# Host-side layouts for the inputs, and the expansion of the softmax weights shared by two engines

## The reference

```
q = layernorm(x) @ Wq.T + bq;  k = ctx @ Wk.T + bk;  v = ctx @ Wv.T + bv
per row (token): reshape q, k, v to 16 heads x 16
  logits[i, j] = q[i] . k[j] / 4        # head i against head j of the SAME row
  out[i] = sum_j softmax_j(logits)[i, j] * v[j]
out: transposed so that heads come before rows, reshaped to (128, 256), @ Wd.T + bd
x = x + out
h = layernorm(x); gates = softmax((h @ w_red) @ normalized(wg).T)   # 8 experts
o = gelu(h @ W1[e] + b1[e]) @ W2[e] + b2[e], e = argmax(gates)      # 256 -> 512 -> 256
x = x + o * max(gates)
```

## Time and profile before

| | |
|---|---|
| Median of 3 runs | 428.82 us (426.50 to 429.31) |
| The profiled execution | 430.04 us |
| Its span, first to last instruction | 428.1 us |
| TensorE busy | 381.1 us, 89% |
| VectorE busy | 310.9 us, 73% |
| POOL busy | 297.2 us, 69% |
| ScalarE busy | 234.8 us, 55% |
| Mean granted clock of TensorE | 0.979 of full speed |
| DMA | 59.31 MB, 97433 packets |

### The profile page before, as it was taken

One profiled execution on the slowest core, in us unless ns is written; L12 is line 12 of the kernel. 1 busy time (PEld: TensorE's weight loads), 2 busy tenths in 40 slices (PEclk: granted clock), 3 DMA queues, 4 the chain that ended last, 5 costly groups with the idle time before them and its releaser, 6 DMA issues.

```text
span 428.1 us, 11390 instructions
## 1 busy us (share of the span) xinstructions
PE 381.1 (89%) x3791; PEld 303.4 (71%) x3791; DVE 310.9 (73%) x667; ACT 234.8 (55%) x783; POOL 297.2 (69%) x399
## 2 busy tenths in 40 slices
PE   6996999999999989998888687978999999999980
PEld 6774676676766657565555466767999999999970
DVE  3746899899998989999999665579456555555640
ACT  4443778787686877776752564571344444444420
POOL 2767678787687877776775964656387777787751
PEclk9999999999999999999999899999899999999996
DMA  7696866978779787886566501131022222222200
GB/s 163 207 264 164 228 173 209 268 193 239 184 211 260 190 229 181 230 209 175 133 155 185 154 27 39 52 116 48 29 64 75 64 75 74 61 69 65 65 17 0
DMA packets 97433, 59.31 MB, mean 139 GB/s; under 512 B 70366, under 2 KB 88447, under 8 KB 97376
## 3 DMA queue, kind: packets, MB, share of 16 engines
...
...
## 4 chain that ended last, share of the span: by engine, by line
PE 34%; DMA 24%; DVE 14%; issue 9%; SPq 9%; POOL 7%; ACT 2%; DVEq 1%; ACTq 0%; POOLq 0%
DMA qkv_scr<-qkv 21%; PE bQ L1107 14%; PE bKV L1075 8%; PE bL L1075 7%; SPq L248 4%; POOL kx L374 3%; SPq L252 2%; SPq L283 2%; DMA b2b<-in_L_ffn_wg 2%; DVE qkv L485 2%; PE bT L1089 2%; DVE qkv L492 1%; DMA ql<-qkv_scr 1%; PE bO L1057 1%; POOL r L420 1%
## 5 line engine op out<-in xcount | busy, mean ns | idle before, releaser
L374 POOL TENSOR_TENSOR kx<-ql,mask 128x2048 f32<-128x2048 f32 x32 | 117.6, 3675 | 42.7 <-issue 32.9
L1107 PE MATMUL bQ<-w,wA 128*128 x312 | 74.3, 381 | 3.4 <-DVE r L721 2.8
L475 DVE TENSOR_TENSOR ax<-bA,mask 128x2048 f32<-128x2048 f32 x32 | 73.3, 2290 | 0.6 <-PE bA L1013 0.6
L1107 PEld LDWEIGHTS bQ<-w,wA 128*128 128x128 f32 x312 | 56.2, 190 | 10.6 <-issue 4.5
L924 PE MATMUL bKV<-wA,xcT 128*128 128x512 f32 x128 | 60.2, 593 | 0.0
L397 POOL DMA_INDIRECT out<-r,isc x39 | 41.3, 1059 | 22.3 <-issue 13.4
L420 POOL DMA_INDIRECT r<-row_scr,ig x39 | 40.5, 1038 | 6.0 <-issue 2.4
L862 ACT ACTIVATE wA<-bL,r 128x128 f32<-128x128 f32 x76 | 21.6, 367 | 41.3 <-PE bL L1075 26.7
L862 ACT ACTIVATE wA<-bKV,r 128x128 f32<-128x128 f32 x80 | 22.8, 367 | 36.1 <-issue 18.8
L355 POOL TENSOR_TENSOR rs<-ve,half 128x2 f32<-128x2 f32 x39 | 28.3, 726 | 20.3 <-ACT ve L742 20.2
L932 PE MATMUL bL<-kx,pad 128*32 128x128 f32 x1024 | 35.8, 282 | 6.8 <-POOL kx L374 6.8
...
## 6 DMA issues: line engine op xcount, KB each, us to landing
...
```

The lines of the kernel that those rows point to most:

```text
L374: eng.tensor_tensor(block(kx[:, z % 2, :]), spread_heads(ql[z % 2][:, :, 0:HD]), mask_b, ALU.mult).then_inc(S["kx"], 1)
L475: eng.tensor_tensor(block(ax[:, :]), spread_heads(bA[:, 0:C].rearrange("p (l i) -> p l i", l=NH)), mask_b, ALU.mult).then_inc(S["ax"], 1)
L1107: i_ = eng.matmul(bQ[:, 0:C], hT[b % 2][:, k, :], w2[:, bass.ds(eb * (KH * C) + k * C, C)], start=(k == 0), stop=(k == KH - 1))
```

## The change

The host now also passes `x` and context transposed, interleaved as `xc` (for each pair of tiles and partition 4 KB in a row), the weights transposed (`wkvT`, `wqT`, `wdT`, `w_redT`, `wgT`), W1 with b1 appended (`W1b`) and W2 as the kernel holds them. `xc` is loaded into `xcT`, which has place for four tiles, two tiles at a time, beside `x` in its own layout. TensorE's turns of tiles and weights and the copies behind them go, with the load of the context. The mean of Wq is now taken off by two matmuls with a matrix of -1/256 (`mean`) and one addition on VectorE. POOL finishes the variance (`ve`) in place of ScalarE, in an instruction of its own whose end it waits for. `SHARE = 3`: of the eight blocks of `ax` VectorE writes the last five, and ScalarE the first three, in three instructions after VectorE's (`scalar_expand`, waits for `ax0`). In ScalarE's step it stands behind the moments of `cat` and ahead of `scalar_ahead` and `oT`. This holds for all 32 tiles.

```diff
--- before.py
+++ after.py
-CT = 6
+XC = 4
...
+SHARE = 3
...
+        xcT = r1[:, 0:XC * 4 * P].rearrange("p (n a c) -> p n a c", n=XC, a=4)
...
-            for w, src in ((1, Wk), (2, Wv), (0, Wq)):
-                eng.dma_start(wst[w], src.rearrange("(a p) c -> p a c", p=P)).then_inc(S[f"ld_w{w}"], 16)
+            eng.dma_start(wT[:, :, 0:2 * C], wkvT).then_inc(S["ld_wkv"], 16)
+            eng.dma_start(wT[:, :, 2 * C:3 * C], wqT).then_inc(S["ld_wq"], 16)
...
-            eng.dma_start(wst[3], Wd.rearrange("(a p) c -> p a c", p=P)).then_inc(S["ld_w3"], 16)
+            eng.dma_start(wst, Wd.rearrange("(a p) c -> p a c", p=P)).then_inc(S["ld_wo"], 16)
+            eng.dma_start(wD[:, :, 0:C], wdT).then_inc(S["ld_wd"], 16)
             eng.dma_start(bdb[:, 0:C], bd.rearrange("(o n) -> o n", o=1).broadcast_to((P, C))).then_inc(S["ld_bd"], 16)
-            eng.dma_start(b1s[:, :], b1.rearrange("e (k p) -> (e k) p", p=P)).then_inc(S["ld_b1"], 16)
...
-                eng.dma_start(w1b[:, n, lo * HID:hi * HID].rearrange("p (k h) -> p k h", h=HID),
-                              W1[n].rearrange("(k p) h -> p k h", p=P)[:, lo:hi, :]).then_inc(S["ld_moe"], 16)
+                lo, hi = lo * HID, hi * HID + (KH if hi == KC else 0)
+                eng.dma_start(w1b[:, n, lo:hi], W1b[n][:, lo:hi]).then_inc(S["ld_moe"], 16)
...
-                    eng.dma_start(xt[:, n % XR:n % XR + 2, 0:C], x[n:n + 2].rearrange("n p c -> p n c")
-                                  ).then_inc(S[f"ld_x{n // 2 % 3}"], 16)
-                    eng.dma_start(ct[:, n % CT:n % CT + 2, :], ctx_in[n:n + 2].rearrange("n p c -> p n c")
-                                  ).then_inc(S[f"ld_c{n // 2 % 3}"], 16)
+                    eng.dma_start(xt[:, n % XR:n % XR + 2, 0:C], x[n // 2]).then_inc(S[f"ld_x{n // 2 % 3}"], 16)
+                c = t + 3 if t > 0 else t + 5 if t == -3 else NT
+                if live(c) and c % 2 == 0:
+                    if c >= XC:
+                        eng.wait_ge(S["qq"], c - XC + 2)
+                    eng.dma_start(xcT[:, c % XC:c % XC + 2, :, :], xc[c // 2]).then_inc(S[f"ld_c{c // 2 % 2}"], 16)
                 if t == -3:
...
-                        eng.wait_ge(S["ve0"], n + 1)
+                        eng.wait_ge(S["va0"], n + 1)
...
-                        eng.wait_ge(S["ve1"], d + 1)
+                        eng.wait_ge(S["va1"], d + 1)
...
+                    eng.tensor_scalar(ve[:, :], va[:, :], 1.0 / C, EPS, ALU.mult, ALU.add).then_inc(S["ve"], 1)
+                    eng.wait_ge(S["ve"], t + 2)
                     eng.tensor_tensor(rs[t % 3][:, :], ve[:, :], half2[:, :], ALU.pow).then_inc(S["rs"], 1)
...
-            eng.tensor_reduce(qsum[:, :], wst[0], AX, ALU.add, negate=True).then_inc(S["wqs"], 1)
-            eng.wait_ge(S["wqs"], 1)
-            eng.scalar_tensor_tensor(wst[0], qsum[:, :].unsqueeze(2).broadcast_to((P, KC, C)), 1.0 / C, wst[0],
-                                     ALU.mult, ALU.add).then_inc(S["wqc"], 1)
...
+            eng.wait_ge(S["wqs"], 1)
+            eng.tensor_tensor(wT[:, :, 2 * C:3 * C], wT[:, :, 2 * C:3 * C],
+                              bX[:, 0:C].unsqueeze(1).broadcast_to((P, KC, C)), ALU.add).then_inc(S["wTq"], 1)
...
-            eng.tensor_tensor(block(ax[:, :]), spread_heads(bA[:, 0:C].rearrange("p (l i) -> p l i", l=NH)),
-                              mask_b, ALU.mult).then_inc(S["ax"], 1)
+            eng.tensor_tensor(block(ax[:, :])[:, :, SHARE:, :],
+                              bA[:, 0:C].rearrange("p (l i) -> p l i", l=NH).unsqueeze(2)
+                              .broadcast_to((P, NH, NB - SHARE, HD)),
+                              mask[:, SHARE:].unsqueeze(1).unsqueeze(3).broadcast_to((P, NH, NB - SHARE, HD)),
+                              ALU.mult).then_inc(S["ax0"], 1)
...
-            eng.activation(ve[:, w:w + 1], va[:, w:w + 1], ACT.Identity,
-                           bias=eps2[:, w:w + 1], scale=1.0 / C).then_inc(S[f"ve{w}"], 1)
-
...
             if live(n):
                 eng.wait_ge(S[f"ld_x{n // 2 % 3}"], (n // 6 + 1) * 16)
                 moments(eng, n, 0, xt[:, n % XR, 0:C])
-            if live(t + 1) and t >= 4:
-                scalar_turned(eng, t + 1)
...
-            eng.dma_start(ct[:, 0, :], ctx_in[0]).then_inc(S["ld_cc"], 16)
-            eng.dma_start(xt[:, 0, 0:C], x[0]).then_inc(S["ld_xx"], 16)
-            eng.wait_ge(S["pad0"], 1)
-            eng.dma_start(wrp[:, :, 0:NG], w_red.rearrange("(a p) g -> p a g", p=P)).then_inc(S["ld_g"], 16)
-            eng.dma_start(wgb, wg.rearrange("e g -> (e g)").rearrange("(o n) -> o n", o=1)
-                          .broadcast_to((P, NE * NG))).then_inc(S["ld_g"], 16)
             with nc.allow_non_contiguous_dma("bd by columns, 256 elements"):
-                eng.dma_start(ct[:, 1, :], ctx_in[1]).then_inc(S["ld_c0"], 16)
-                eng.dma_start(xt[:, 1, 0:C], x[1]).then_inc(S["ld_x0"], 16)
-                eng.dma_start(bdc[:, :], bd.rearrange("(a p) -> p a", p=P)).then_inc(S["ld_bc"], 16)
+                eng.dma_start(xcT[:, 0, :, :], xc[0][:, 0, :, :]).then_inc(S["ld_cc"], 16)
+                eng.dma_start(xt[:, 0, 0:C], x[0][:, 0, :]).then_inc(S["ld_xx"], 16)
+                eng.dma_start(wrT, w_redT).then_inc(S["ld_g"], 16)
+                eng.dma_start(wgT[:, :], wgT_in).then_inc(S["ld_g"], 16)
+                eng.dma_start(wgb, wg.rearrange("e g -> (e g)").rearrange("(o n) -> o n", o=1)
+                              .broadcast_to((P, NE * NG))).then_inc(S["ld_g"], 16)
+                eng.dma_start(xcT[:, 1, :, :], xc[0][:, 1, :, :]).then_inc(S["ld_c0"], 16)
+                eng.dma_start(xt[:, 1, 0:C], x[0][:, 1, :]).then_inc(S["ld_x0"], 16)
+                eng.dma_start(bdc[:, :], bd_col).then_inc(S["ld_bc"], 16)
...
                     moments(eng, w, 1, cat[w % CR][:, 0:C])
+                if live(s1):
+                    scalar_expand(eng, s1)
                 if t >= 5:
                     scalar_ahead(eng, t)
...
+        def scalar_expand(eng, s1):
+            eng.wait_ge(S["ax0"], s1 + 1)
+            for b in range(SHARE):
+                i_ = eng.activation(block(ax[:, :])[:, :, b, :], bA[:, 0:C].rearrange("p (l i) -> p l i", l=NH), ACT.Copy,
+                                    scale=mask[:, b:b + 1])
+            i_.then_inc(S["ax"], 1)
...
+        def tensor_weights(eng):
+            eng.wait_ge(S["ld_wq"], 16)
             for k in range(KC):
-                i_ = eng.transpose(bY[:, k * P:(k + 1) * P], wrp[:, k, :], ident[:, :])
-            i_.then_inc(S["wrt"], 1)
-
-        def tensor_weights_gate(eng):
+                i_ = eng.matmul(bX[:, 0:C], mean, wT[:, k, 2 * C:3 * C], start=(k == 0), stop=(k == KC - 1))
+            i_.then_inc(S["wqs"], 1)
...
                 i_ = eng.matmul(bY[:, C + k * NE:C + (k + 1) * NE], wrc[0:NG, k, :], wgT[:, :], start=True, stop=True)
             i_.then_inc(S["gmm"], 1)
...
+                eng.wait_ge(S[f"ld_c{a // 2 % 2}"], (a // 4 + 1) * 16)
...
-            if live(a + 1):
-                tensor_turned(eng, a + 1)
             if a == 1:
                 tensor_gate(eng)
-                weight_transposes(eng, 3)
...
+def laid_out(inputs, np):
+    def blocks(w, n):
+        return w.reshape(n, P, -1).transpose(1, 0, 2)
...
+    xc = np.stack((x.reshape(NT, P, KC, P), ctx.reshape(NT, P, KC, P)), 2).transpose(0, 4, 2, 3, 1)
+    return {
+        "x": x.reshape(NT // 2, 2, P, C).transpose(0, 2, 1, 3),
+        "xc": xc.reshape(NT // 2, 2, P, 4, P).transpose(0, 2, 1, 3, 4),
+        "wkvT": np.concatenate((blocks(i["Wk"].T, KC), blocks(i["Wv"].T, KC)), 2),
+        "wqT": blocks(i["Wq"].T, KC),
+        "wdT": blocks(i["Wd"].T, KC),
...
+        "bd_col": i["bd"].reshape(KC, P).T,
+        "w_redT": i["w_red"].T,
+        "wgT": i["wg"].T,
...
+        "W1b": np.concatenate((i["W1"].reshape(NE, KC, P, HID).transpose(0, 2, 1, 3).reshape(NE, P, KC * HID),
+                               i["b1"].reshape(NE, KH, P).transpose(0, 2, 1)), 2),
+        "W2": i["W2"].reshape(NE, KH, P, C).transpose(0, 2, 1, 3).reshape(NE, P, KH * C),
```

More of the change, by code:

```diff
@@ L51 @@
 B2_PARTS = 4
+SHARE = 3
 SELR = NH2 + 2
 PIECES = (("oh_a", 1), ("rv_a", 5), ("rv_a", 10), ("rv_a", 13), ("texp_a", 1), ("selk_a", 1), ("taken_a", 1))
-SEMS = ("ld_xx ld_cc ld_x0 ld_x1 ld_x2 ld_c0 ld_c1 ld_c2 st_q0 st_q1 ld_q0 ld_q1 st_r0 st_r1 st_r2 st_r3 st_r4 ld_w0 ld_w1 ld_w2 ld_w3 ld_g ld_b ld_bd "
-        "ld_b1 ld_bc ld_moe ld_b2 pad0 filled ident iotas const zeroed mask nmax gpow wrt ctr0 ctr bdm gmm gate gx gxs "
-        "wtr wTk wTv wTq wTd wqs wqc gsq nr2 wgd wide tr_in xT qq kv kvad qad xb kx pad qk mx lsub exp sm rsm norm tr_a ax pvo oT wd x2 nb gm gsub "
-        "scaled score nm0 nm1 va0 va1 ve0 ve1 pw rs rsd oh cnt rv selr selp selk invmm texp idg ids ig isc yo yb "
+SEMS = ("ld_xx ld_cc ld_x0 ld_x1 ld_x2 ld_c0 ld_c1 st_q0 st_q1 ld_q0 ld_q1 st_r0 st_r1 st_r2 st_r3 st_r4 ld_wq ld_wkv ld_wd ld_wo ld_g ld_b ld_bd "
```

(32 more changed lines are left out.)

118 lines of the change are left out of this document (25 added, 93 removed).

## The result

The changed kernel takes 452.04 us (median of four runs, 450.31 to 453.71) against 428.93 for the kernel before (four runs, 426.50 to 429.31): a ratio of 1.055, 95% interval 1.049 to 1.061. I forecast 438 and a range of 423 to 445. The direction was right, and the price of 23 us was two and a half times mine. The profiled execution took 450.31, the fastest of its four, while that of the kernel before (430.04) was slower than its median. Its span is 448.5 against 428.1, so 20.4 us are to be found between the two traces.

What follows compares the result with a forecast made beforehand. SyncE's loop was taken to bound the ordinary steps by half a microsecond, VectorE those from step 24. Terms +0.5 + 2.5 - 5.2 + 11.4 = +9.2 us on 430.04 gave 439.2, set to 438 for the median; range 423 to 445.

Steps and rivals of the forecast that it cites:

- Start, +0.5: Before the first store: weight transposes go, some 0.5 MB more are loaded; +0.5 us, ends -3 and +2.
- the loads, +2.5: SyncE's loads up to 172 us: `xc` brings 256 KB more per pair of steps, 0.26 us each; +2.5 us.
- rival C: Transfers cost their full time, 1.0 us a pair, and the store lands late each time: 445 us; chance 0.10.
- Ordinary steps, 0: Ordinary steps: the loop over `ax` becomes 6.4 us, still covered by SyncE's loop of 6.73; no change.
- Steps 24 to 30, -5.2: VectorE leads in these seven steps and 0.80 us of each goes; two with wide loads give back 0.4; -5.2 us.
- Steps 32 to 35, +11.4: Drain steps: `bO` now waits for ScalarE's share behind the moments, delaying TensorE's later work; +11.4 us, ends 0 and +13.
- A: Drain costs half, +5 instead of +11.4, ScalarE's late steps being partly covered: 431 to 432 us; chance 0.17.
- B: Faster: POOL paces steps 32 to 34, `bO`'s delay stays within its slack, `xc` fits idle DMA: 424 us; chance 0.21.
- D: Steps 24 to 30 gain nothing, the loop over `ax` with routing work leading there: 443 us; chance 0.10.

Runs made afterwards that it cites:

- e2: Changed kernel with its host layouts, but VectorE expands the whole of `ax` in every step; 437.87 us, ratio 1.018.
- e4: Changed kernel, VectorE expanding all of `ax`, loading only the context's half of the wide load (256 KB per pair of steps instead of 512); 429.13 us, ratio 0.999.
- e9: Changed kernel, VectorE expanding all of `ax`, wide load kept, experts' weight halves issued two at a time in the even steps; 430.80 us, ratio 1.002.
- e5: Changed kernel, but the transposed arrays load one tile (256 KB) in every step instead of two in every second; 444.92 us, ratio 1.035.
- e8: Changed kernel with host layouts, one tile of transposed arrays loaded a step, ScalarE's share in steps 24 to 30 alone; 428.01 us, ratio 0.998.
- e12: Changed kernel with one tile of the transposed arrays a step and VectorE alone expanding in steps 32 to 35; 429.80 us, ratio 1.002.
- e11: Changed kernel, but in steps 32 to 35 TensorE does 44 further transposes before it waits for `ax`; 446.39 us, ratio 1.038.
- e7: Changed kernel, but in steps 32 to 35 ScalarE does its share at the head of its step; 438.24 us, ratio 1.019.
- e1: Changed kernel, but in steps 32 to 35 VectorE expands the whole of `ax`; 435.21 us, ratio 1.0105.
- e10: e8 with the experts' halves issued two at a time in the even steps, as in e9; 426.78 us, ratio 0.995.
- e6: Kernel before, with ScalarE's share of three blocks in steps 24 to 30 alone; 427.64 us, ratio 0.9935.

## Why the prediction was right in direction and wrong in size

**Start, +0.5: right, as far as it can be told.** +0.2. The other kernels with the layouts lie between -2.1 and +1.1 at step 5, and the two without them at -0.6 and -2.7, so one trace does not tell +0.5 from nothing.

**The first step that failed: the loads, +2.5, measured +7.9.** I priced the wide load by its bytes, 0.26 us a pair of steps from the loops of the earlier trace rows, and put the issue of the half at nothing: it "waits for `ql`'s descriptors, not its own. Nothing." A pair costs 0.88, and the layouts alone 8.7 us by the medians (e2). e4 and e9 show that nearly all of it comes from 512 KB with a half behind them in one step: take 256 KB away, or move the half, and it is gone. That issue stood in the chain of waits before the change already, `SPq L248` with 4% and `SPq L252` with 2%, and its duration in the steps around 100 to 120 us of that trace goes from 1.24 to 2.14 us. One instruction of one size that varies like this is being held up. Behind `ql` alone it takes 1.2 us and behind another half 0.43 (e9), so there is a wait for `ql`'s descriptors as I wrote; but behind the wide load it took 1.39 to 4.17 us, and the queue's next instruction is the store. Of the 1.13 us that the odd step grew, 0.70 lie there and 0.43 in the landing of the store. I had not priced the landing of `ql` either, which the chain goes through.

The size I allowed as rival C, 1.0 us a pair. But its mechanism, that the bytes cost their full time on the DMA engines wherever they stand, falls with e5, e8 and e9. The Trainium skill says that the time of the issuing engine to start a DMA is "usually small relative to the DMA itself" (DMA: Bandwidth & Descriptors, Issuing engines are not separate DMA queues); here it was up to 4.53 us in e2, where the median of these transfers from issue to landing is 4.5 to 5.3 us. The page also advises larger single transfers for bandwidth (Rules for kernel authors); here one tile of 256 KB in each step beat two of them in one transfer of 512 KB by 7.1 us, for what stands in the queue next and not for bandwidth. What in the queue holds the issue back (entries, bytes or the order of descriptors) no run here separates.

**Ordinary steps, 0: nearly right.** The loop over `ax` is 6.4 us as worked out. I compared it with the mean of 6.73, and the mean covers steps that are shorter: 7 of the 19 steps from 5 on took 6.23 to 6.31 us before. Raised to 6.41 they cost 1.1 us; e12 against e8 shows 1.8, not well separated from nothing.

**Steps 24 to 30, -5.2: too much.** -2.7 measured, 7.3 us a step and not 6.9, and 1.5 to 3.7 gained between the starts of steps 24 and 31 in the ten traces with the share there. The three traces without it gain 0.2 to 1.2 as well, so the share's own part is smaller still. VectorE is the bound in most of these steps, but not in each. Its longest wait in e8 from 169.5 to 220 us (us in total, times, longest):

```profile
DVE r L575 <- PE bY L977: 1.2, 1, 1.2
```

and its starts there, steps 25 to 28:

```profile
177.06 1.49 DVE L467 TENSOR_TENSOR ax<-bA,mask 128x1280 f32<-128x1280 f32 x1
185.19 1.49 DVE L467 TENSOR_TENSOR ax<-bA,mask 128x1280 f32<-128x1280 f32 x1
191.87 1.49 DVE L467 TENSOR_TENSOR ax<-bA,mask 128x1280 f32<-128x1280 f32 x1
199.00 1.49 DVE L467 TENSOR_TENSOR ax<-bA,mask 128x1280 f32<-128x1280 f32 x1
```

Step 25 takes 8.13 us, against 8.04 before: there the routing's counts on TensorE stand behind the wait for `ax`, which ScalarE now ends, and VectorE waits 1.2 us for them. Step 26 takes 6.68 against 7.51 and gains its 0.8 whole. I multiplied 0.80 by seven without following who waits for `ax` in each step. Why steps 24, 27 and 30 gain only 0.2 to 0.3 in e8 was not tried. In the changed kernel the wide load reaches into this stage as well: step 27 takes 8.76 us there against 7.35 before and 7.13 in e8, after an issue of a half that took 4.17 us (at 196.03) and a `ql` that took 6.8 us to land.

**Steps 32 to 35, +11.4: mechanism right, but the second step that failed is here, size short by 3.9.** The lateness of each `bO`, less what the kernel had at the expansion of step 32:

| `bO` of step | forecast | after | e11, clock kept | e7, share first | e1 |
|---|---|---|---|---|---|
| 32 | 5.3 | 5.2 | 5.2 | 3.0 | 0.0 |
| 33 | 4.9 | 6.7 | 5.6 | 1.5 | 0.5 |
| 34 | 10.1 | 12.6 | 10.1 | 2.9 | 0.4 |
| 35 | 11.4 | 15.3 | 10.9 | 2.0 | 0.4 |

With the clock kept the working from the earlier trace rows holds to 0.7 us in every step. It took TensorE's durations from rows at full clock, 1.1 us for each `bO`, although it itself put waits of several microseconds ahead of them, and the trace of before had the half clock after such a wait (240.73 above). The rest, 15.3 less 10.9, is the half clock, 4.4 us in the traces and 5.6 in the medians. The Trainium skill has the rule that TensorE should have no idle gaps between bursts of matmuls, or its clock drops (TensorE: Matmul & The Clock Gate, Why this matters for your kernels); the trace agrees, 1.93 us for 1.08. A wait does not always bring the clock down, though: the same 2.92 us ahead of the last `bO` in kernels with VectorE alone there were followed by 1.08 us in five traces (the kernel before, e2, e8, e9, e10) and by 1.58 to 1.94 in four (e1, e4, e6, e12).

**The rivals.** A and B fall: `bO` of step 33 is 6.7 us late, above the 3.7 at which B decides, and nothing of the delay is taken back later. C had the size of the loads and not their mechanism. D is half right for steps 24 to 30.

**The sum again** with what the runs showed: 0.2 + 7.9 - 2.9 + 15.3 - 0.1 = 20.4. Two effects missing from my list, a wide load that holds up what stands behind it in its queue and a clock that falls in a wait I had myself forecast, make 5.4 and 3.9 of the 11 us by which I was short between the traces; steps 24 to 30 make the other 2.3, less 0.4 at the start and the end. By the medians I was short by 14.
